# A mixture-of-experts phase in which TensorE issues the gate and up products two pairs ahead

## The reference

```
def _experts(x_flat, Wg, Wu, Wd):
    g = silu(einsum('nc,eci->nei', x_flat, Wg))
    u = einsum('nc,eci->nei', x_flat, Wu)
    return einsum('nei,eic->nec', g * u, Wd)

shared = mean(_experts(xf, sWg, sWu, sWd), axis=1)      # one shared expert
probs = softmax(xf @ Wgate + expert_bias)               # 8 experts
topk_p, topk_i = top_k(probs, 2)
topk_p = topk_p / sum(topk_p)
comb = sum(one_hot(topk_i, 8) * topk_p[..., None], axis=1)
routed = einsum('ne,nec->nc', comb, _experts(xf, Wg, Wu, Wd))
return shared + routed
```

## Time and profile before

| | |
|---|---|
| median of 3 runs | 1758.8 us (1750.39, 1758.8, 1761.38) |
| profiled execution | 1753.17 us, span of its instructions 1751.4 us |
| granted TensorE clock, mean of the span | 0.948 of full speed |
| experts phase | from 1023.1 us to about 1211.7 us of the span |

### The profile page before, as it was taken

One profiled execution on the slowest core, in us unless ns is written; L12 is line 12 of the kernel. 1 busy time (PEld: TensorE's weight loads), 2 busy tenths in 40 slices (PEclk: granted clock), 3 DMA queues, 4 the chain that ended last, 5 costly groups with the idle time before them and its releaser, 6 DMA issues. The chain is left out here.

```text
span 1751.4 us, 35791 instructions
## 1 busy us (share of the span) xinstructions
PE 1554.5 (89%) x12174; PEld 672.5 (38%) x12174; DVE 1305.9 (75%) x2453; ACT 1123.2 (64%) x1781; POOL 595.4 (34%) x1081
## 2 busy tenths in 40 slices
PE   5899999689599999999999789887689999999787
PEld 3422222244244444444443655444323333333232
DVE  6699999778777777777772446775889999999064
ACT  7699999545155565555566343433468888888656
POOL 6334434577322313223221001212423332333474
PEclk9799999889699999999999999998779999999898
DMA  8734435358311212122110500000722222232201
GB/s 237 166 63 66 73 62 133 71 116 212 74 33 41 53 33 63 44 53 54 33 44 14 181 24 1 0 1 30 214 44 51 49 48 47 53 54 72 63 14 48
DMA packets 88813, 119.66 MB, mean 68 GB/s; under 512 B 23957, under 2 KB 61973, under 8 KB 88422
## 3 DMA queue, kind: packets, MB, share of 16 engines
q1 hardware_dynamic: 87030, 115.94, 27.9%
q10 hardware_dynamic: 1616, 1.54, 0.3%
HBM read 69.74 MB, written 47.58 MB: 67 GB/s over the span
## 5 line engine op out<-in xcount | busy, mean ns | idle before, releaser
L1290 DVE TENSOR_REDUCE o_sb<-ps 128x1 f32<-128x512 f32 (+3 forms) x810 | 662.9, 863 | 130.1 <-PE ps L1092 123.9
L1185 ACT ACTIVATE q_buf<-ps 128x1024 f32<-128x1024 f32 (+1 forms) x768 | 574.2, 909 | 201.5 <-PE ps L1063 200.3
L1185 ACT ACTIVATE pr_buf<-ps 128x1024 f32<-128x1024 f32 (+1 forms) x384 | 293.0, 908 | 63.3 <-PE ps L1063 63.1
L1114 PE MATMUL ps<-q_buf,v_buf 128*9 128x512 f32 (+7 forms) x2880 | 307.7, 518 | 5.3 <-DVE q_buf L1342 2.3
L1246 POOL TENSOR_SCALAR_AFFINE_SELECT q_buf<-q_buf 128x256 f32<-128x256 f32 (+1 forms) x360 | 176.9, 509 | 394.3 <-ACT q_buf L1185 295.7
L1063 PE MATMUL ps<-q_buf 48*128 48x512 bf16 (+7 forms) x1536 | 278.3, 333 | 30.5 <-ACT q_buf L1185 9.6
L1246 POOL TENSOR_SCALAR_AFFINE_SELECT pr_buf<-pr_buf 128x256 f32<-128x256 f32 (+1 forms) x280 | 134.4, 502 | 301.7 <-ACT pr_buf L1185 230.7
L1063 PE MATMUL ps<-q_buf,k_buf 49*128 49x512 f32 (+3 forms) x1152 | 207.7, 487 | 0.0
L1063 PEld LDWEIGHTS ps<-q_buf 48*128 48x128 bf16 (+1 forms) x1536 | 83.7, 94 | 274.9 <-ACT q_buf L1185 152.6
L1342 DVE TENSOR_SCALAR q_buf<-q_buf 128x1024 f32<-128x1024 f32 x192 | 162.1, 876 | 12.1 <-ACT q_buf L1185 8.1
L1114 PE MATMUL ps<-pr_buf,v_buf 128*9 128x512 f32 (+7 forms) x1728 | 157.2, 456 | 2.3 <-POOL pr_buf L1246 1.4
(11 more groups left out here) (223 smaller groups left out, 1935.7 us busy)
## 6 DMA issues: line engine op xcount, KB each, us to landing
qm_d<-pr_buf SPq DMA_DIRECT2D x80, 128.0 KB, 2.4
q_buf<-qm_d SPq DMA_DIRECT2D x24, 384.0 KB, 5.7
o_d<-pr_buf SPq DMA_DIRECT2D x16, 512.0 KB, 2.6
q_buf<-o_d SPq DMA_DIRECT2D x8, 1024.0 KB, 5.1
q_d<-q_buf SPq DMA_DIRECT2D x48, 128.0 KB, 2.2
k_d<-q_buf SPq DMA_DIRECT2D x48, 128.0 KB, 2.1
q_buf<-q_d SPq DMA_DIRECT2D x62, 96.0 KB
q_buf<-k_d SPq DMA_DIRECT2D x62, 96.0 KB
```

The source lines that it names most:

```text
L1114: mm = nc.tensor.matmul(ps[VW * j:VW * j + V_ROWS_OUT, o_bank + half % O_BUFS, lo * P:(lo + nq) * P], v, units(i, r, j)[:, 0, off * P:(off ...
L1185: nc.scalar.activation(units(i, g, WIDE * e, WIDE), ps[:, bank:bank + WIDE, :], ACT.Exp, scale=scale).then_inc(s_e, 1)
L1290: nc.vector.tensor_reduce(to, sc, AX_X, ALU.max).then_inc(s_mr, 1)
```

## The change

The two products of a pair become a function, `gate_up`. In the loop over the ten pairs of a sequence the broadcast product of pair m is issued first and the gate and up products of pair m + 2 behind it. Pairs 0 and 1 of a sequence are issued earlier, ahead of `turn_gates`: for sequences 1 to 3 behind the down products of the sequence before, for sequence 0 in `front`, where four of nine fills are taken out. The waits of each product are the same as before. The lists of the other engines are not changed.

```diff
+            AHEAD = 2
...
+                    def gate_up(b, u, j):
+                        n = 2 * GP * b + GP * u + j
+                        rows = P if j < PAIRS else INNER
+                        r = (GP * u + j) % 2
+                        pe.wait_ge(s_h, n + 1 + BASE)
+                        nc.tensor.matmul(ps[0:rows, 2 + r, :], w_sb["wg"][:, j * P:j * P + rows],
+                                         xrT[:, u, :], start=True, stop=True)
+                        nc.tensor.matmul(ps[0:rows, 4 + r, :], w_sb["wu"][:, j * P:j * P + rows],
+                                         xrT[:, u, :], start=True, stop=True).then_inc(s_gu, 1)
+
                     def front(b):
                         fill(7, 6)
                         logits(b)
-                        fill(7, 9)
+                        for j in range(AHEAD):
+                            gate_up(b, 0, j)
+                        fill(7, 5)
                         pe.wait_ge(s_tab, 2)
                         turn_gates(b)
 
                     def body(b, following):
-                        for u in range(2):
-                            pe.wait_ge(s_cc, 2 * b + u + 1 + BASE)
-                            for j in range(GP):
-                                n = 2 * GP * b + GP * u + j
-                                rows = P if j < PAIRS else INNER
-                                r = (GP * u + j) % 2
-                                pe.wait_ge(s_h, n + 1 + BASE)
-                                nc.tensor.matmul(ps[0:rows, 2 + r, :], w_sb["wg"][:, j * P:j * P + rows],
-                                                 xrT[:, u, :], start=True, stop=True)
-                                nc.tensor.matmul(ps[0:rows, 4 + r, :], w_sb["wu"][:, j * P:j * P + rows],
-                                                 xrT[:, u, :], start=True, stop=True).then_inc(s_gu, 1)
-                                if j < PAIRS:
-
-                                    pe.wait_ge(s_hc, PAIRS * (2 * b + u) + j + BASE)
-                                    nc.tensor.matmul(ps[:, 0, :], spread[0:SPLIT, j * P:(j + 1) * P],
-                                                     combT[0:SPLIT, u, :], start=True, stop=True).then_inc(s_cb, 1)
+                        for m in range(2 * GP):
+                            u, j = divmod(m, GP)
+                            if j == 0:
+                                pe.wait_ge(s_cc, 2 * b + u + 1 + BASE)
+                            if j < PAIRS:
+                                pe.wait_ge(s_hc, PAIRS * (2 * b + u) + j + BASE)
+                                nc.tensor.matmul(ps[:, 0, :], spread[0:SPLIT, j * P:(j + 1) * P],
+                                                 combT[0:SPLIT, u, :], start=True, stop=True).then_inc(s_cb, 1)
+                            if m + AHEAD < 2 * GP:
+                                gate_up(b, *divmod(m + AHEAD, GP))
                         if following is not None:
                             logits(following)
...
                         if following is not None:
+                            for j in range(AHEAD):
+                                gate_up(following, 0, j)
                             turn_gates(following)
```

## The result

The changed kernel takes 1774.1 us (median of 6 runs, 1770.8 to 1776.3) where the kernel before took 1754.5 us (6 runs, 1750.4 to 1761.4). The recorded ratio is 1.0087, 95% interval 1.0064 to 1.0110: some 15 us slower (the two medians by themselves are 19.6 us apart, and a repeat on another occasion gave 1.0083). I go by the ratio, since the runs of before spread over 11 us. The forecast was 1760 with a range to 1769.

A forecast was written before the change was run, and what follows sets the result against it. TensorE sets the pace, so only its idle time, about 11 us, could be won. Terms of +0.4, +1.9 and +2.5 summed to +4.8 us; from the mean of 1755.9 that gave 1760.7, forecast as 1760, range 1750 to 1769.

The forecast's parts named there:

- Part 1: Sequence restart: pair 2 at E + 8.49 us in sequences 1 to 3 (E: TensorE's down products done); sum +0.4 us.
- Part 2 and 3: From pair 2 to a sequence's end, with 0.98 us of new idle time before the transposes; sum +1.9 us.
- Rival (d): VectorE's loop lacks the 0.25 us slack per step, so pairs wait for its product: 1769 us; chance 0.10.
- Part 4: TensorE's clock: falls to 1.2 GHz in three of four sequences against one now, +2.5 us.
- the rival (c): Clock falls in all sequences, one of them into the 12 us of down products: 1766 us; chance 0.15.
- The bound of +8.2 us: Upper bound of the clock's cost: falls in four sequences, one reaching the down products, 3 x 1.7 + 3.1 us.
- (a): Restart costs nothing and all 8.7 us of waits at the broadcast product vanish: 1747 us; chance 0.07.
- (b): Nothing comes of it: pair wait conditions are unchanged, the holes merely move: 1755 to 1757 us; chance 0.18.

The follow-up runs named there:

- the order alone: Changed kernel with pairs 0 and 1 back behind the turns of the gates and nine fills in front again; ratio 1.0017 against the kernel before, median 1762.5 us.
- the new order with fills: Changed kernel, but pairs 0 and 1 behind the turns, with fills ahead of the transposes, between them and between the turns; ratio 0.9968 against before, median 1751.5 us.
- before filled: Kernel before with fills between the transposes, between the turns of the gates and behind pair 1; ratio 0.9981 against the kernel before.
- the change with the end filled: Changed kernel with one fill ahead of the next sequence's transposes, the restart hole left as it is; ratio 1.0057 against the kernel before.
- the pairs ahead alone: Kernel before with pairs 0 and 1 moved ahead of the turns, each later pair still ahead of its broadcast; ratio 1.0043 against the kernel before.
- the restart alone filled: Changed kernel with three fills behind each sequence's first broadcast product, the hole before the transposes left; ratio 1.0051 against the kernel before.
- the end hole in the kernel before: Kernel before with each sequence's last broadcast product issued behind pair 9 instead of ahead of it; ratio 1.0013 against the kernel before.
- both holes filled: Changed kernel with three fills behind each sequence's first broadcast product and one ahead of the next transposes; ratio 1.0034 against before, median 1761.4 us.
- the new order with the end filled: Changed kernel, but pairs 0 and 1 behind the turns, with only the one fill ahead of the transposes; ratio 0.9975 against the kernel before.
- the change filled: Changed kernel with fills in both new holes, between the two transposes and between the turns; ratio 1.0010 against the kernel before.
- down products in the hole: Changed kernel, pairs 0 and 1 behind the turns, first down product tile ahead of the transposes, fills between transposes and between turns; ratio 0.9974 against before.

## Why the prediction was wrong

**Part 1, restart: right.** Forecast pair 2 at E + 8.49, measured E + 8.41, 8.40 and 8.41; sequence 0 4.85 behind the turn, measured 4.87. The chain is ScalarE's copies, table load and SiLU, as said. The table load costs 1.28 us and shows no drain behind it: the copy ends at 1093.01 and the first SiLU starts at 1094.33. What I did not see is that moving the pairs ahead undid a gain of the new order inside the sequence: without the move pair 2 comes 0.95 us earlier than before (the order alone), with it 1.1 us later in sequence 1 and within 0.2 us of the old place in sequences 2 and 3.

**Part 2 and 3, order and end: right.** Forecast 17.85 us from pair 2 to the transposes; where the clock is at 1.00 it is 17.77 (1130.82 to 1148.59 in the new order with fills). The wait at pair 8 is there (0.28 us shown, forecast 0.63), the hole ahead of the transposes is 1.03 us shown for 0.98. Rival (d) did not come: in sequence 0 no pair behind pair 2 waits, so VectorE's loop fits in its slack.

**Part 4, the clock: this step failed.** It put "falls in three of four sequences against one now: 2 x 1.24 = +2.5 us", where the runs leave 12 to 13 us. The places and the kind of cost were right; the term was mis-sized in three ways. First the count and the price at the restarts: all four fell, in both profiles of the change. They cost 6.9 us in the first (the length from pair 2 to the end less the forecast without clock: 1.9, 1.5, 2.3, 1.2) and 10.1 in the repeat, against 1.2 in the profile of before. Second, the hole of 1.0 us ahead of the transposes was priced at its length only. Behind it come the transposes, a gap of 0.96 us, the logits and 12 us of down products. This stretch ran at the low clock in part in all three sequences and grew by 12.1 us in the first profile and 6.0 in the repeat; the rival (c) allowed for one stretch of down products at 3.1 us. The prediction's own sign of being wrong, the low clock in the down products more often than once, came true. Third, the base: I took the number of falls of before from one execution, and that number differs from one execution to the next, as the spread of 1749 to 1768 us in the runs of before shows. I also took the length of the hole as what decides between a fall and none; the runs don't bear that out (last section). The bound of +8.2 us should have been the sum over every stretch of PE that follows a new hole: four restarts at 1.7 and three stretches at 4 to 5, some 20 us, and 1776 would have been in the range.

That the clock, and not the order by itself, makes most of the loss is shown by the kernel with every hole filled: same order, +1.8 us instead of +15, and some +5 against the kernel before filled likewise. How the loss divides between the two holes is not shown. Filling one at a time saves 5 and 6 us with intervals of 4 to 5. Each half of the change alone costs +7.5 us (pairs ahead) and +3 us (order), and the hole ahead of the transposes put into the kernel before costs +2.3. Which executions fall, and when, is not shown either.

**The rivals.** (a) and (b) failed, (c) was the right mechanism with too small a price. The ratio stayed within 1% with little to spare, and the direction was right.

## What to carry to other kernels

Work moved ahead of a wait is a gain only if the waiting chain itself doesn't pass behind it: here two pairs of 3.5 us stood in front of four small products on which ScalarE's copies, table load and SiLU hung, and the same reordering without that move, its gaps filled, was 5.6 us faster than before. When TensorE sets the pace, give every new gap two prices, its length and what follows it at half clock, and take the sum over all stretches behind gaps as the bound; a cheap fill in the gap, also in the kernel before, tells the two costs apart. One profile gives the structure exactly but the clock only as one sample of many: compare clock losses over many runs.

## What the runs showed of the hardware

Holes of 2.6 to 3.8 us at the restart had 1.2 GHz behind them in all sixteen sequences of four profiles (the change and its repeat, the change with the end filled, the pairs ahead alone), from the first product on or within the next 2 us. Holes of 1.15 us in the order alone had none in three of three sequences (pair 2 to the end took 17.77, 17.77 and 16.57 us there). In between, length does not decide: the hole of 2.42 us in sequence 2 of before had no fall behind it, and the one of 2.04 us in the new order with fills had a granted clock of 0.65 in the 4.4 us behind it.

The down products show the same. Each profile has three stretches of them that can be slow, 12.0 us at full clock:

| gaps of TensorE ahead of them | profiles | at full clock |
|---|---|---|
| 1.03 us and 0.96 us | the change, its repeat, the restart alone filled, the order alone, the end hole in the kernel before | 0 of 15 |
| 0.96 us alone | before, both holes filled, the end alone filled, the pairs ahead alone, the new order with the end filled | 4 of 15 |
| both filled | before filled, the change filled, the new order filled, down products in the hole | 7 of 12 |

So the low clock came although TensorE was never idle there for more than 1.03 us at a time, closing the gaps made it rarer, and 5 of 12 were slow even so. What decides in the single case stays open.

In the kernel before with fills the nine fills of the front ended 1.7 us sooner, at full clock, and so left a longer wait for the gates:

```profile
1043.55 0.61 PE L2105 MATMUL ps<-ident_bf,q_buf 128*72 128x128 bf16 x4 [3.33 <-issue]
```

The turns then ran at 1.2 GHz (0.61 us for 0.39). The new order with fills has the same hole and turns at full speed behind it:

```profile
1042.49 0.39 PE L2106 MATMUL ps<-ident_bf,q_buf 128*72 128x128 bf16 x4 [3.31 <-issue]
```

A faster stretch ahead of a wait makes the hole longer, and it can bring the low clock there instead.
